# The node update's two products as pairs of half-array matmuls, with the rectified copies in pairs

## What is computed

```python
for l in range(L):                      # L = 3
    h = _ln(x, n1g[l], n1b[l])
    ...                                 # q, k, v per edge; softmax per target node; agg
    gate = jax.nn.sigmoid(agg @ Wih[l] + bih[l] + h @ Whh[l] + bhh[l])
    upd = agg + gate * (h @ Wself[l] + bself[l] - agg)
    x = x + upd @ Wout[l] + bout[l]
    h2 = _ln(x, n2g[l], n2b[l])
    x = x + jax.nn.relu(h2 @ mW1[l] + mb1[l]) @ mW2[l] + mb2[l]
```

## Time and profile before

| | |
|---|---|
| time, median of 3 runs | 9080.73 us (9078.8 to 9091.13) |
| the profiled execution, its own time | 9078.37 us |
| its span, first to last instruction | 9076.6 us |
| POOL busy | 6367.0 us (70%) |
| DVE busy | 5796.4 us (64%) |
| PE busy | 3144.1 us (35%), 9857 instructions |
| ACT busy | 2850.5 us (31%) |
| mean granted TensorE clock | 0.662 of full speed |

### The profile page before, as it was taken

How to read it: one execution, slowest core, us unless ns; L and a number is a source line. 1 busy time by engine, 2 the same in 40 slices (tenths; PEclk the granted TensorE clock), 3 DMA queues, 4 the chain that set the end, 5 groups by cost and what they waited for, 6 DMA issues and landing times.

```text
span 9076.6 us, 45051 instructions
## 1 busy us (share of the span) xinstructions
PE 3144.1 (35%) x9857; PEld 1808.8 (20%) x9857; DVE 5796.4 (64%) x6109; ACT 2850.5 (31%) x2181; POOL 6367.0 (70%) x6734
## 2 busy tenths in 40 slices
PE   2555455553222222222432222222352222223325
PEld 1111111111122212222222122222221122222212
DVE  1777766775376677667446776677644766776673
ACT  1666666664122222222212222222231222222223
POOL 6777777775577777777367777777727777777762
PEclk9877777776666666666766656665675666656657
DMA  3655555553343344333143443344314433443331
GB/s 53 208 177 185 193 192 178 177 186 128 126 150 132 132 140 150 132 132 132 55 136 132 140 150 132 132 140 150 116 49 139 150 132 132 140 149 133 132 110 49
DMA packets 405487, 1247.08 MB, mean 137 GB/s; under 512 B 196101, under 2 KB 253910, under 8 KB 360006
## 3 DMA queue, kind: packets, MB, share of 16 engines
q0 software_dynamic: 215104, 429.19, 17.5%
q1 hardware_dynamic: 169606, 468.24, 14.7%
q10 hardware_dynamic: 20736, 349.23, 9.6%
HBM read 808.34 MB, written 437.84 MB: 137 GB/s over the span
## 4 chain that ended last, share of the span: by engine, by line
POOL 68%; issue 23%; PE 3%; DVE 2%; DVEq 1%; DMA 1%; ACT 1%; POOLq 0%; SPq 0%; ACTq 0%
POOL G L545 64%; POOL qexp L595 1%; PE PS L773 1%; POOL QQ L584 1%; PE PS L777 1%; POOL s2exp L564 1%; POOL G L584 1%; POOL S L551 1%; PE PS L722 0%; DVEq L1453 0%; DVE EA L1375 0%; ACT EA L942 0%; PE PS L766 0%; DVE SX L1445 0%; PE PS L767 0%
## 5 line engine op out<-in xcount | busy, mean ns | idle before, releaser
L545 POOL DMA_INDIRECT G<-tabkv,srcI x4704 | 4438.3, 944 | 1433.5 <-issue 1433.5
L752 PE MATMUL PS<-Wkvp,EA 128*128 128x256 f32 x4704 | 1640.9, 523 | 4328.9 <-DVE PX L1429 4251.3
L752 PEld LDWEIGHTS PS<-Wkvp,EA 128*128 128x128 f32 x4704 | 1232.5, 270 | 4737.9 <-DVE PX L1429 4416.1
L545 POOL DMA_INDIRECT G<-tab,srcI x1568 | 1480.9, 944 | 508.0 <-issue 501.2
L955 ACT ACTIVATE QQ<-QQ 128x3584 f32<-128x3584 f32 x84 | 538.0, 6405 | 3313.3 <-DVE PX L1429 3062.7
L1426 DVE TENSOR_TENSOR PS<-PS,G 128x512 f32<-128x512 f32 x588 | 408.5, 695 | 1593.0 <-DMA G<-tabkv,srcI 1584.1
L969 ACT ACTIVATE S<-SX 128x4480 f32<-128x4480 f32 x81 | 663.6, 8193 | 1238.6 <-DVEq L1453 1238.6
L1415 DVE TENSOR_TENSOR_SCAN QQ<-PS,QQ 128x456 f32<-128x456 f32 x672 | 679.7, 1084 | 210.0 <-ACT QQ L955 194.4
L1452 DVE TENSOR_TENSOR_SCAN SX<-PS,SX 128x456 f32<-128x456 f32 x756 | 763.4, 1084 | 12.2
L1429 DVE TENSOR_TENSOR PX<-PS,QQ 128x512 f32<-128x512 f32 x588 | 624.8, 1063 | 43.8
L693 PE MATMUL PS<-hid,W2raw 128*64 128x512 f32 x1568 | 479.3, 712 | 342.6 <-ACT hid L882 333.6
(11 more groups left out here) (308 smaller groups left out, 4073.5 us busy)
## 6 DMA issues: line engine op xcount, KB each, us to landing
st<-S ACTq DMA_DIRECT2D x81, 2240.0 KB, 7.8
EA<-eaT SPq DMA_DIRECT2D x84, 1792.0 KB, 7.8
QQ<-qexp SPq DMA_DIRECT2D x84, 1792.0 KB, 7.4
st<-S ACTq DMA_DIRECT2D x27, 3668.0 KB
G<-tabkv,srcI POOLq DMA_INDIRECT x4704, 2.5
xe<-in_edge_attr SPq DMA_DIRECT2D x28, 1792.0 KB, 7.4
qexp<-zeros SPq DMA_DIRECT2D x28, 1792.0 KB, 11.3
eaT<-eaC ACTq DMA_DIRECT2D x28, 1792.0 KB
```

What stands on the lines that cost most here:

```text
L545: nc.gpsimd.indirect_dma_start(out=G[:, u, t, :], out_offset=None, in_=tab[:, :], in_offset=IND(ap=srcI[:, u, t:t + 1], axis=0)).then_inc( ...
L752: last = mm(PS[:, b + j // 2, 2 * P * (j % 2):2 * P * (j % 2) + 2 * P], EA[:, u, 4 * s + j, :], Wkvp[:, :], start=True, stop=True)
```

## The change

`hidden(kh)` takes one weight tile mW1s of 128 columns whose rows hold the same weights twice, and issues two matmuls: rows 0 to 63 into one PSUM bank, rows 64 to 127 into another (`HBANK` gives the two banks of each block). `folded` issues its four matmuls with 64 weight columns each, q = 0 onto partitions 0 to 63 and q = 1 onto partitions 64 to 127 of the block's bank. No weight tile has padding, so the two weight tiles shrink to a half and a quarter, two memsets go, and SP loads mW2 in two transfers a layer where it took four. On ACT a step makes two rectified copies, one from each bank, with one wait ahead of the pair and one increment behind it. PE has 9 steps and ACT 6.

```diff
-NTW, NLW = 19, 30
+NTW, NLW = 19, 28
-B_PE, B_ACT, B_DVE = 11, 8, 5
+B_PE, B_ACT, B_DVE = 9, 6, 5
+HBANK = [(k, k + 3) if k < 3 else (k, (k + 4) % 8) for k in range(NB)]
...
-        mW1s = sb("mW1s", [P, 2, HID])
-        mW2s = sb("mW2s", [P, 2, 2, P])
+        mW1s = sb("mW1s", [P, HID])
+        mW2s = sb("mW2s", [P, 2, D])
...
-                    mat(l, mW1s[rows, q, :], "mW1", l_w)
-                    for kh in range(2):
-                        mat(l, mW2s[:, kh, q, q * D:(q + 1) * D], "mW2", l_w, slice(kh * P, (kh + 1) * P))
+                    mat(l, mW1s[rows, :], "mW1", l_w)
                 for kh in range(2):
+                    mat(l, mW2s[:, kh, :], "mW2", l_w, slice(kh * P, (kh + 1) * P))
...
-                def hidden(kh, q):
-                    return lambda k, c0, w: mm(PS[:, k, 0:w], mW1s[:, q, kh * P:(kh + 1) * P], nB5[:, c0:c0 + w], start=True, stop=True)
+                def hidden(kh):
+
+                    def step(k, c0, w):
+                        for q in range(2):
+                            rows = slice(q * D, (q + 1) * D)
+                            last = mm(PS[:, HBANK[k][q], 0:w], mW1s[rows, kh * P:(kh + 1) * P], nB5[rows, c0:c0 + w], start=True, stop=True)
+                        return last
+                    return step
 
                 def folded(k, c0, w):
                     for n, src in enumerate(HIDDEN):
-                        last = mm(PS[:, k, 0:w], mW2s[:, n // 2, n % 2, :], src[:, c0:c0 + w], start=(n == 0), stop=(n == 3))
+                        kh, q = n // 2, n % 2
+                        last = mm(PS[q * D:(q + 1) * D, k, 0:w], mW2s[:, kh, :], src[:, c0:c0 + w], start=(kh == 0), stop=(kh == 1))
                     return last
...
-                    on(half, hidden(0, 0), b_dve, B, B_DVE, 3)
-                    for n in range(1, 4):
-                        on(half, hidden(n // 2, n % 2), b_act, A_, B_ACT, 3 + n)
-                    on(half, folded, b_act, A_, B_ACT, 7)
+                    on(half, hidden(0), b_dve, B, B_DVE, 3)
+                    on(half, hidden(1), b_act, A_, B_ACT, 4)
+                    on(half, folded, b_act, A_, B_ACT, 5)
...
-                    for n in range(4):
-                        on(half, lambda k, c0, w: f(HIDDEN[n][:, c0:c0 + w], PS[:, k, 0:w], ACT.Relu, bias=mb1c[:, n // 2:n // 2 + 1]),
-                           b_pe, P_, B_PE, 6 + n)
+                    for kh in range(2):
+
+                        def units(k, c0, w):
+                            for q in range(2):
+                                last = f(HIDDEN[2 * kh + q][:, c0:c0 + w], PS[:, HBANK[k][q], 0:w], ACT.Relu, bias=mb1c[:, kh:kh + 1])
+                            return last
+                        on(half, units, b_pe, P_, B_PE, 6 + kh)
...
-            for block_weights in (Wkvp[:, :], Wqkv[:, :], Wn[:, :, :], mW1s[:, :, :], mW2s[:, :, :, :]):
+            for block_weights in (Wkvp[:, :], Wqkv[:, :], Wn[:, :, :]):
...
-                    on(half, onto_x(MB2), b_pe, P_, B_PE, 10)
+                    on(half, onto_x(MB2), b_pe, P_, B_PE, 8)
```

## The result

The changed kernel takes 9016.31 us (median of 4 runs, 9015.28 to 9030.34), the kernel before 9079.76 us (4 runs): a ratio of 0.9931, 95% interval 0.9914 to 0.9948. The forecast was 9019 us, range 9008 to 9036. The profiled execution of the changed kernel is the longest of its four, 9030.34 us; its span is 9028.5 us.

What follows compares the result with a forecast made beforehand. GpSimd's gathers were taken to bound the kernel, with the two products on the path; savings of 9.7 and 10.65 us a half, 20.35 a layer, 61 over three layers gave 9019 us, range 9008 to 9036.

Steps and rivals of the forecast that it cites:

- What bounds, and the path: GpSimd's gathers hold 64% of the chain; the products' six stretches, 143 us, lie on it with no edge loop beside.
- Part 1: PE, `hidden` and `folded`: a pair costs one full matmul, saving 10.3 us in first halves, 11.2 us in second.
- Part 2: ACT's copies of `hidden` results: two per pair, costing PE 0.35 us in the first half, which takes 12.8 us.
- The second half: `hidden` and `folded` in a layer's second half: 14.1 us with ACT, plus 0.25 for tiling changes, where 25.0 stood.
- Part 3: PE's changes of tiling, `hidden` to `folded` and `folded` to full matmuls: 0.25 us a half, 1.5 us over six.
- Part 4: PE's fewer waits for `hidden` gain zero; `sums` ends 9.4 us in, so `turned` gets no new wait.
- Part 5: SP's two fewer transfers a layer are hidden, 0; the two dropped memsets at the start give 0, at most 1 us.
- the clock stays low past the products: Rival: PE's steps behind the products, such as gates and next means, run at the low clock; 36 us slower, 9117; 2%.
- The sum: Savings in the layer updates: 9.7 us first half, 10.65 second, 20.35 a layer, 61 us over three layers.
- The last point named as wrong: Sign against the forecast: edge loop times differing by more than 1 us, which nothing in it accounts for.
- The rise named there for 4 to 5 us: Sign for the forecast: PE's clock rises 4 to 5 us into a stretch of `hidden` and `folded`.

Runs made afterwards that it cites:

- memsets_back: The changed kernel with two memsets of the unpadded weight tiles put back at the program's start; PE's idle time ahead of `hidden` 5.36 us, no total given.
- after_again: The changed kernel run again unchanged, beside the kernel before: 9034.73 us, ratio 0.9935.
- copies_only: The changed kernel's step order, banks and paired copies, but both products as full matmuls with padded weights: 9094.87 us, ratio 1.0 against the kernel before.

## Why the prediction was right

- **What bounds, and the path.** Right. The pieces of the update are saved where they stand, and the difference of the medians, 63.4 us, is matched by the sum of the table's rows, 63. That the path has nothing beside it was the step that the whole forecast rested on.
- **Part 1, a pair for the price of one.** Right for both forms: `folded` 5.30 us where six slots of 0.86 make 5.2, and each form alone gave half.
- **Part 2, ACT.** The first half was forecast at 12.8 us and 0.25 for the tiling; it is 12.81, 12.78, 12.74, and that for a rise of the clock 0.9 us earlier than assumed, worth 0.4 us; with a rise at 4.3 (memsets_back, layer 1) it is 12.87. ACT's price of 0.35 us a half was measured as 0.2 and 0.5. Before the change I had priced all three layers by the 22.75 us of layer 0; those of the others are 0.2 and 0.3 us longer.
- **The second half** is the mis-sized term: 14.1 and 0.25 forecast, 13.5 measured. The forecast rested on a rise of the clock at about 5.0 us, from the rows of before; it came at 2.9, and half of 2.1 us is 1.05. When it came at 3.7 (after_again, layer 2) the stretch took 13.87, at 4.7 (memsets_back, layer 0) 14.09. The rise was treated as a property of the stretch, and it isn't one.
- **Part 3, drains.** `folded` with 5.30 us to the next transposes has 0.15 over six slots. The Trainium skill's drain on a change of tiling mode ("TensorEngine Tiling (Array Packing)", Key Properties) costs that little here, from 64-column pairs to full matmuls. The other change of each half, `hidden` to `folded`, can't be read apart from ACT's copies, so the 0.25 us a half is borne out only in part.
- **Part 4, no new wait.** `sums` ends 9.45 us into the stretch (4480.78), `folded` at 12.8: right. What I called hidden at zero in **Part 5** had a side effect: without the two memsets DVE stalls for 0.45 us in each layer.
- **The rival "the clock stays low past the products"** happened in a small way: the clock falls later than the gates, for 3.4 us, and costs 1.0 us a layer there. But it doesn't need the pairs: copies_only shows it with full matmuls, after_again is without it in one layer. What decides it is open. The Trainium skill ("TensorE: Matmul & The Clock Gate", Part 1) says that the monitor behind the clock runs freely and doesn't start with the kernel; the moments of the rise seen here, which move between 2.8 and 6.1 us after the start of like stretches, agree.
- The sum was 61 us, the table has 63. The terms off are, a layer, +1.0 us for the middle and 0.45 for DVE, against -0.4 in the first and -1.0 in the second half and about -0.7 in the first piece, where the clock rises 3.4 to 3.6 us behind the last transposes and not 4.1, 5.0 and 5.2. That they nearly cancel is luck, and with it that the forecast came within 3 us; the stretches themselves, 65.3 us less where 61 were forecast, were off by 4. The last point named as wrong, edge loops that differ by more than 1 us, did occur in the profiled execution (4 us a loop), and lies in GpSimd's issue time in that run. The rise named there for 4 to 5 us was off too.
